# Values' and output projections of an attention and mixture-of-experts block as three half-precision products

## The chip, the cores and the metric

The kernel runs on one core of a Trainium2 chip. The metric is the device time of one execution in microseconds (us). A difference is judged against the spread of repeated runs.

## What is computed

For each of 8 sequences of 512 tokens with 256 features the reference computes attention with 32 heads of 8 features, and then a feed-forward layer with 2 shared and 16 routed experts, of which each token takes 4. A layer norm follows each of the two. Cut to what matters here:

```
q = rope(x @ Wq.T);  k = rope(x @ Wk.T);  v = x @ Wv.T
allowed = causal & (4 chunks of 32 keys, by q against the chunk's mean k)
o = softmax(where(allowed, q k' / sqrt(8), -1e30)) @ v
o = o * rsqrt(mean(o*o)) * o_norm_weight * sigmoid(x @ Wg1.T @ Wg2.T)
x = layernorm(x + o @ Wo.T)
x = layernorm(x + ffn(x))
```

q and k decide which chunks are chosen. v and Wo only scale the result.

## The kernel before

The weights stay on the chip. Eight turns follow, one for each sequence b. Turn b holds the attention of b and, woven into it, the feed-forward layer of m = b - 1. All engines run fixed programs and meet through semaphores; the order of the work is that in which each engine's program is written. A turn has these stages:

- the first products: the transpose of the normed tokens (`x1_transpose`), the transposes and chunk means of q and k, the router, and the experts' first chunks;
- the choice of chunks: DVE finds the best chunks, PE and ACT stack q and k (`stack`), and the experts' chunks 3 to 10 run beside them;
- the maxima: 40 units, in which PE makes the scores (`max_unit`) and DVE reduces them (L1346); between them the experts' chunks 11 to 21 go through PE (`up`, `down`), ACT (L834, L843), DVE (L1156) and POOL (L1045, the `low` part);
- the probabilities: 8 groups of 5 units, in which PE makes the scores again (`key_unit`, L503), ACT takes their exponentials (L986), POOL masks them (L1105) and PE multiplies by v (`outputs`, L712);
- the junction to turn b + 1, which the change touches.

In the junction PE's program is, in this order: `project_v(b + 1, 0)` (L399), `to_tokens(NG - 2)` (L722), the last group's `outputs`, `heads_out(0)` (four transposes of the gated heads, L760, into the PSUM bank `BK_AT`), `to_tokens(NG - 1)`, `project_qk` for token tiles 0 and 1 (L407), `project_v(b + 1, 1)`, `heads_out(1)` into the same bank, `project_out(0)` and `(1)` (L767), `project_qk` and `project_v` for tiles 2 and 3. In the meantime DVE normalises the last groups of heads (`two_groups`, ending in L1391), turns q and k of tiles 0 and 1 (`rope`, L1244 and L1245), adds x to the projected output (L1409), and does the layer norm (L1178 to L1188), whose result PE transposes at L512. ACT copies the transposed heads from PSUM to `aT` (`heads_copy`, L995), with the products of `turned` (L892, L893: 16 for each pair of tiles) between the copy of k = 0 and that of k = 1, and then copies v (L899).

A product of 32-bit operands stands in the trace as two MATMUL records, one of 16-bit operands as one. The experts' products already use pairs of 16-bit parts: three products (high by high, high by low, low by high) take the place of one.

At the start DVE fills a few buffers (L1132 to L1136), turns q and k of the first tiles (L1242 to L1245), and takes the low parts of the experts' weights (L1418, L1143), while PE projects sequence 0. In the last turn no next sequence is projected: PE goes from `to_tokens(NG - 1)` straight to `heads_out(1)`.

## Time and profile before

| | |
|---|---|
| median of 3 runs | 1489.6 us (1489.12 to 1492.46) |
| the profiled execution: its time, its span | 1490.47 us, 1488.7 us |
| PE busy | 1349.9 us (91%) in 11024 matmuls |
| DVE busy | 1085.1 us (73%) |
| ACT busy | 840.4 us (56%) |
| POOL busy | 533.7 us (36%) |
| mean granted TensorE clock | 0.956 |

The span is the stretch from the first to the last instruction in the trace. A busy share is a mean over stages with different limits, so what an edit is worth has to be read from the stage in which it stands. Matmuls overlap, so that PE counts as busy while it waits for little else than the end of the last one.

### The profile page before, as it was taken

How to read it: one execution, taken by the hardware profiler on the slowest of the kernel's cores; microseconds unless marked ns; L12 is line 12 of the kernel's file. 1: busy time of each engine (PE TensorE's matmuls, PEld its weight loads, DVE VectorE, ACT ScalarE, POOL GpSimd, SP SyncE). 2: the span in 40 equal slices, each digit the busy share in tenths (PEclk: the TensorE clock that was granted, in tenths of full speed). 3: DMA queues.
4: the chain of work that ended last, by engine and by line, in shares of the span. 5: the costliest groups of instructions: out<-in, count | busy, mean ns of one | idle time of the engine just before them, and what ended most of it. 6: DMA issues, size and time to landing. Idle time of an engine off the chain costs nothing.

```text
span 1488.7 us, 29120 instructions
## 1 busy us (share of the span) xinstructions
PE 1349.9 (91%) x11024; PEld 740.0 (50%) x11024; DVE 1085.1 (73%) x2746; ACT 840.4 (56%) x1266; POOL 533.7 (36%) x638
## 2 busy tenths in 40 slices
PE   5687999999998999989999999989999899999697
PEld 3322565536654465535755356543654357553364
DVE  6993679857797578966789577975789667985534
ACT  5407773396635865287733966358752776339221
POOL 3203532254223542245322553235322453225143
PEclk8657999999999999999999999999999999999799
DMA  6001031200221021210222003211112102220031
GB/s 235 15 15 16 15 91 61 51 30 23 80 70 36 25 65 57 66 31 15 87 64 51 16 23 93 64 37 30 61 56 71 31 16 72 64 52 16 16 111 60
DMA packets 52207, 77.74 MB, mean 52 GB/s; under 512 B 6322, under 2 KB 26724, under 8 KB 51812
## 3 DMA queue, kind: packets, MB, share of 16 engines
q1 hardware_dynamic: 52068, 75.89, 17.5%
q8 instruction: 87, 1.43, 0.4%
q14 instruction: 52, 0.43, 0.1%
HBM read 66.95 MB, written 8.65 MB: 51 GB/s over the span
## 4 chain that ended last, share of the span: by engine, by line
PE 54%; DVE 22%; ACT 12%; issue 4%; DVEq 3%; POOL 2%; DMA 2%; SPq 0%; POOLq 0%
PE PS L568 12%; PE PS L556 12%; DVE CM L1346 8%; ACT UQ L986 7%; PE PS L712 7%; PE PS L486 4%; DVE hr L1156 3%; PE PS L503 3%; PE PS L456 3%; ACT UK L986 2%; POOL hp L1045 2%; PE PS L767 2%; PE PS L722 2%; PE PS L407 2%; DVEq L1148 1%
## 5 line engine op out<-in xcount | busy, mean ns | idle before, releaser
L1045 POOL TENSOR_TENSOR hp<-hr,hp 128x512 f16<-128x512 f32 (+1 forms) x200 | 236.9, 1184 | 623.6 <-ACT hp L843 560.3
L1346 DVE TENSOR_REDUCE CM<-PS 128x32 f32<-128x1024 f32 x320 | 377.3, 1219 | 29.3 <-PE PS L486 25.2
L568 PE MATMUL PS<-W,hp 128*128 128x256 f16 (+1 forms) x2400 | 315.1, 274 | 16.2 <-POOL hp L1045 15.7
L556 PE MATMUL PS<-x1T,W 128*128 128x512 f16 (+1 forms) x1200 | 314.2, 389 | 0.0
L568 PEld LDWEIGHTS PS<-W,hp 128*128 128x128 f16 (+1 forms) x2400 | 214.2, 98 | 104.0 <-POOL hp L1045 38.2
L843 ACT ACTIVATE hp<-hr 128x512 f16<-128x512 f32 (+1 forms) x178 | 112.7, 633 | 247.2 <-DVE hr L1156 229.7
L834 ACT ACTIVATE hr<-PS,CF 128x512 f32<-128x512 f32 (+1 forms) x200 | 137.0, 685 | 198.3 <-PE PS L556 193.0
L1156 DVE TENSOR_TENSOR hr<-hr,gB 128x512 f32<-128x512 f32 x176 | 126.1, 717 | 103.0 <-ACT hr L834 99.7
L556 PEld LDWEIGHTS PS<-x1T,W 128*128 128x128 f16 (+1 forms) x1200 | 108.7, 100 | 115.0 <-issue 38.7
L986 ACT ACTIVATE UK<-PS 128x1024 f32<-128x1024 f32 x160 | 153.4, 1041 | 10.8 <-PE PS L503 10.5
L986 ACT ACTIVATE UQ<-PS 128x1024 f32<-128x1024 f32 x160 | 150.4, 1042 | 1.6
L503 PE MATMUL PS<-qET,kz 64*128 64x512 f16 (+3 forms) x1024 | 111.5, 304 | 27.5 <-ACT UK L986 12.0
L486 PE MATMUL PS<-kz,qET 64*128 64x512 f16 (+3 forms) x1024 | 132.5, 318 | 0.0
L1105 POOL TENSOR_SCALAR_AFFINE_SELECT UK<-UK 128x512 f32<-128x512 f32 x128 | 78.6, 639 | 148.3 <-ACT UK L986 148.3
L503 PEld LDWEIGHTS PS<-qET,kz 64*128 64x128 f16 x1024 | 32.1, 94 | 165.8 <-ACT UQ L986 70.3
L1364 DVE COPY ropeb<-PS 128x512 f32<-128x512 f32 x64 | 44.3, 692 | 93.8 <-PE PS L712 93.6
L1105 POOL TENSOR_SCALAR_AFFINE_SELECT UQ<-UQ 128x512 f32<-128x512 f32 x128 | 78.8, 640 | 65.9 <-ACT UQ L986 65.9
L712 PE MATMUL PS<-UK,vst 128*9 128x512 f32 (+3 forms) x1024 | 87.6, 437 | 0.0
L712 PE MATMUL PS<-UQ,vst 128*9 128x512 f32 (+3 forms) x1024 | 83.9, 434 | 0.0
L930 ACT ACTIVATE kz<-PS 128x1024 f16<-128x1024 f16 x64 | 65.2, 1018 | 6.8 <-PE PS L456 6.8
L477 PE MATMUL PS<-CG 128*128 128x256 bf16 x256 | 52.2, 288 | 17.1 <-DVE CM L1346 16.9
L933 ACT ACTIVATE qET<-PS 128x1024 f16<-128x1024 f16 x64 | 65.7, 1027 | 0.0
(149 smaller groups left out, 1803.4 us busy)
## 6 DMA issues: line engine op xcount, KB each, us to landing
gB<-gates SPq DMA_DIRECT2D x64, 256.0 KB, 3.2
gB<-gates SPq DMA_DIRECT2D x32, 224.0 KB, 2.9
gB<-gates SPq DMA_DIRECT2D x32, 192.0 KB, 2.9
gB<-gates SPq DMA_DIRECT2D x32, 160.0 KB, 2.5
xT<-in_xT SPq DMA_DIRECT2D x8, 512.0 KB, 5.5
qET<-rows SPq DMA_DIRECT2D x16, 256.0 KB, 5.4
v<-in_x SPq DMA_DIRECT2D x8, 512.0 KB, 4.1
gB<-gates SPq DMA_DIRECT2D x32, 128.0 KB, 2.9
```

The lines of the kernel that those rows point to most:

```text
L486: mm = pe.matmul(PS[:, r + half, o:o + w], qET[rows, a, t * P:(t + 1) * P], kz[rows, a, 0:w], start=False, stop=True, skip_group_check=Tru ...
L503: mm = pe.matmul(PS[:, r + half, o:o + w], kz[rows, a, t * P:(t + 1) * P], qET[rows, a, t * P:S], start=True, stop=True, tile_position=(64 ...
L556: mm = pe.matmul(PS[0:w, BK_H[c % 2], :], W1[:, a, k, bass.ds(f0, w)], x1T[:, e, k, :], start=(n == 0), stop=(n == 5))
L568: mm = pe.matmul(PS[:, BK_Y + j // 2, (j % 2) * D:(j % 2 + 1) * D], hp[0:w, slot, a, j * P:(j + 1) * P], W2[0:w, e, bass.ds(c, 1), :].rear ...
L712: mm = pe.matmul(PS[32 * hh:32 * hh + HD + 1, BK_PV, t * P:S], vst[:, gs % 2, t, hh, :], PT[gs % 2][:, hh, o:o + w], start=(n == 0), stop= ...
L834: nc.scalar.activation(hr[0:w, slot, :], PS[0:w, BK_H[c % 2], :], ACT.Relu, bias=bias).then_inc(act_h, 1)
L843: nc.scalar.activation(hp[0:w, slot, 0, :], hr[0:w, slot, :], ACT.Copy).then_inc(s_high, 1)
L986: nc.scalar.activation(dst, src, ACT.Exp, scale=SCALE).then_inc(act_p, 1)
L1045: nc.gpsimd.tensor_tensor(hp[0:w, slot, 1, :], hr[0:w, slot, :], hp[0:w, slot, 0, :], ALU.subtract).then_inc(pool_hp, 1)
L1105: nc.gpsimd.affine_select(block, block, [[0, HG], [1, P]], ALU.is_ge, zero, base=0, channel_multiplier=-1).then_inc(pool_p, 1)
L1156: nc.vector.tensor_tensor(hr[:, slot, :], hr[:, slot, :], gB[:, r, :], ALU.mult).then_inc(dve_h, 1)
L1346: nc.vector.tensor_reduce(dst, src, AX.X, ALU.max).then_inc(dve_cm, 1)
```

## The change

The projection of v and the output projection, so far one product of 32-bit operands for each token tile and half of the contraction, become three products of 16-bit parts. The weights are multiplied by 64 before they are split, and the results divided by 64 as they leave PSUM (in ACT's copy of v and in DVE's addition of x). The parts of the weights are made once, at the start, by DVE and ACT, in the place of the 32-bit weights, with 64 times the weights held for a time in the unused end of `kz`. The input is split for each sequence: `high_x` on ACT and `low_x` on POOL, behind chunks 5 and 6 of the maxima of the turn before, and at the start for sequence 0. The transposed heads are split by `heads_copy` on ACT (high) and a new `heads_low` on DVE (low), which reads the PSUM bank as well. The projections of q and k stay as they are. At the start they now stand ahead of those of v.

```diff
@@ -49,6 +49,8 @@
+WIDE = 64.0
@@ -131,6 +133,7 @@
+        xTp = sb("xTp", [P, 2, KT, S], F16)
@@ -156,9 +159,12 @@
-        aT = qf[:, 0:1024].rearrange("p (k s) -> p k s", k=KT)
+        aTp = qf[:, 0:1024].bitcast(F16).rearrange("p (e k s) -> p e k s", e=2, k=KT)
         ropew = qf[:, 1024:3072].rearrange("p (t c) -> p t c", t=NT)
         kz = sb("kz", [P, H // 2, S], F16)
+        wide_w = kz[:, :, :].rearrange("p a s -> p (a s)").bitcast(F32)[:, 12 * D:16 * D].rearrange("p (n k d) -> p n k d", n=2, k=KT)
+        WVp = WA[:, :, 2 * D:3 * D].bitcast(F16).rearrange("p k (e d) -> p e k d", e=2)
+        WOp = WO[:, :, :].bitcast(F16).rearrange("p k (e d) -> p e k d", e=2)
@@ -394,15 +405,17 @@
                 if j == 0:
-                    pe.wait_ge(s_xT, 16 * b + 16)
-                for k in range(KT):
-                    mm = pe.matmul(PS[:, BK_Y + j // 2, (j % 2) * D:(j % 2 + 1) * D], xT[:, k, j * P:(j + 1) * P],
-                                   WA[:, k, 2 * D:3 * D], start=(k == 0), stop=(k == KT - 1))
+                    pe.wait_ge(act_xh, b * KT + KT)
+                    pe.wait_ge(pool_xl, b * KT + KT)
+                for n, (k, a, e) in enumerate((k, a, e) for k in range(KT) for a, e in ((0, 0), (0, 1), (1, 0))):
+                    mm = pe.matmul(PS[:, BK_Y + j // 2, (j % 2) * D:(j % 2 + 1) * D], xTp[:, a, k, j * P:(j + 1) * P],
+                                   WVp[:, e, k, :], start=(n == 0), stop=(n == 3 * KT - 1))
...
+                pe.wait_ge(s_xT, 16 * b + 16)
@@ -410,8 +423,10 @@
                 for j in range(first, last):
+                    project_qk(b, j)
+                pe.wait_ge(dve_wide, 2)
+                for j in range(first, last):
                     project_v(b, j)
-                    project_qk(b, j)
@@ -755,7 +770,7 @@
                     if k:
-                        pe.wait_ge(act_aT, b * KT + k)
+                        pe.wait_ge(dve_aT, b * KT + k)
@@ -763,11 +778,16 @@
-                    for j in range(NT):
-                        mm = pe.matmul(PS[:, 4 + j // 2, (j % 2) * D:(j % 2 + 1) * D], aT[:, k, j * P:(j + 1) * P],
-                                       WO[:, k, :], start=(k == 0 and j % 2 == 0), stop=(k == KT - 1), skip_group_check=True)
-                        if j % 2 and k == KT - 1:
-                            mm.then_inc(pe_att, 1)
+                    for a, parts in ((0, (0, 1)), (1, (0,))):
+                        if a:
+                            pe.wait_ge(dve_aT, b * KT + k + 1)
+                        for j in range(NT):
+                            for e in parts:
+                                mm = pe.matmul(PS[:, 4 + j // 2, (j % 2) * D:(j % 2 + 1) * D], aTp[:, a, k, j * P:(j + 1) * P],
+                                               WOp[:, e, k, :], start=(k == 0 and a == 0 and j % 2 == 0 and e == 0),
+                                               stop=(k == KT - 1 and a == 1), skip_group_check=True)
+                            if j % 2 and k == KT - 1 and a == 1:
+                                mm.then_inc(pe_att, 1)
@@ -814,6 +834,15 @@
+            def high_x(b, k):
+                act.wait_ge(s_xT, 16 * b + 16)
+                nc.scalar.activation(xTp[:, 0, k, :], xT[:, k, :], ACT.Copy).then_inc(act_xh, 1)
+            for k in range(KT):
+                high_x(0, k)
+            act.wait_ge(dve_wide, 1)
+            nc.scalar.activation(WVp[:, 0], wide_w[:, 0], ACT.Copy).then_inc(act_wide, 1)
@@ -897,7 +926,7 @@
-                                     ACT.Copy).then_inc(act_v, 1)
+                                     ACT.Copy, scale=1.0 / WIDE).then_inc(act_v, 1)
@@ -945,6 +974,8 @@
+                        if more and u in (5, 6):
+                            high_x(b + 1, u - 5)
@@ -992,7 +1023,7 @@
-                    nc.scalar.activation(aT[:, k, :], PS[:, BK_AT, :], ACT.Copy).then_inc(act_aT, 1)
+                    nc.scalar.activation(aTp[:, 0, k, :], PS[:, BK_AT, :], ACT.Copy).then_inc(act_aT, 1)
@@ -1014,6 +1045,8 @@
+            act.wait_ge(dve_wide, 3)
+            nc.scalar.activation(WOp[:, 0], wide_w[:, 1], ACT.Copy).then_inc(act_wide, 1)
@@ -1034,6 +1067,13 @@
+            def low_x(b, k):
+                pool.wait_ge(act_xh, b * KT + k + 1)
+                nc.gpsimd.tensor_tensor(xTp[:, 1, k, :], xT[:, k, :], xTp[:, 0, k, :], ALU.subtract).then_inc(pool_xl, 1)
+            for k in range(KT):
+                low_x(0, k)
@@ -1082,12 +1122,16 @@
-                    for (first, last), steps in ((C_TOPK, NG // 2), (C_MAX, MAX_STEPS)):
-                        n = (last - first) // steps
-                        pool.drain()
-                        for i in range(0, steps):
-                            for u in range(n):
-                                low(m, i * n + first + u, (first + u) % 2)
+                    pool.drain()
+                    for c in range(*C_TOPK):
+                        low(m, c, c % 2)
+                    pool.drain()
+                for u, c in enumerate(range(*C_MAX)):
+                    if m is not None:
+                        low(m, c, c % 2)
+                    if more and u in (5, 6):
+                        low_x(b + 1, u - 5)
+                if m is not None:
@@ -1129,6 +1173,9 @@
+            nc.vector.tensor_scalar(wide_w[:, 0], WA[:, :, 2 * D:3 * D], WIDE, None, ALU.mult).then_inc(dve_wide, 1)
+            dve.wait_ge(act_wide, 1)
+            nc.vector.tensor_tensor(WVp[:, 1], wide_w[:, 0], WVp[:, 0], ALU.subtract).then_inc(dve_wide, 1)
@@ -1307,7 +1354,8 @@
-                    nc.vector.tensor_scalar(WO[:, :, :], WO[:, :, :], onw, None, ALU.mult).then_inc(dve_w, 1)
+                    dve.wait_ge(act_wide, 2)
+                    nc.vector.tensor_tensor(WOp[:, 1], wide_w[:, 1], WOp[:, 0], ALU.subtract).then_inc(dve_w, 1)
@@ -1399,15 +1447,22 @@
+                def heads_low(k):
+                    dve.wait_ge(act_aT, b * KT + k + 1)
+                    nc.vector.tensor_tensor(aTp[:, 1, k, :], PS[:, BK_AT, :], aTp[:, 0, k, :], ALU.subtract).then_inc(dve_aT, 1)
+                heads_low(0)
                 if more:
                     rope(b + 1, 0, 2)
+                heads_low(1)
...
-                    nc.vector.tensor_tensor(x1n[:, 2 * i:2 * i + 2, :].rearrange("p t d -> p (t d)"), PS[:, 4 + i, :],
-                                            x[:, 2 * i:2 * i + 2, :].rearrange("p t d -> p (t d)"), ALU.add).then_inc(dve_x1, 1)
+                    nc.vector.scalar_tensor_tensor(out=x1n[:, 2 * i:2 * i + 2, :].rearrange("p t d -> p (t d)"), in0=PS[:, 4 + i, :],
+                                                   scalar=1.0 / WIDE, in1=x[:, 2 * i:2 * i + 2, :].rearrange("p t d -> p (t d)"),
+                                                   op0=ALU.mult, op1=ALU.add).then_inc(dve_x1, 1)
@@ -1416,6 +1471,8 @@
+            dve.wait_ge(s_small, 16 * N_SMALL)
+            nc.vector.tensor_scalar(wide_w[:, 1], WO[:, :, :], onw, WIDE, ALU.mult, ALU.mult).then_inc(dve_wide, 1)
...

```

PE's program in the junction, from `project_v(b + 1, 0)` on, with the products of v (L399) and of the output (L767); before:

```order
L399 MATMUL PS<-WA,xT 128x256 x2
L760 MATMUL PS<-CF,qT 128x128 [waits act_aT,dve_on,act_p]
L760 MATMUL PS<-CF,qT 128x128 x3
L767 MATMUL PS<-WO,qET 128x256 [waits dve_otok,act_aT]
L767 MATMUL PS<-WO,qET 128x256 x3
L767 MATMUL PS<-WO,qET 128x256 [waits dve_otok,act_aT]
L767 MATMUL PS<-WO,qET 128x256 x3
```

and in the changed kernel, where these lines are L411, L775 and L786:

```order
L411 MATMUL PS<-WA,xTp 128x256 x6
L775 MATMUL PS<-CF,qT 128x128 [waits dve_aT,dve_on,act_p]
L775 MATMUL PS<-CF,qT 128x128 x3
L786 MATMUL PS<-WO,qET 128x256 [waits dve_otok,act_aT]
L786 MATMUL PS<-WO,qET 128x256 x7
L786 MATMUL PS<-WO,qET 128x256 [waits dve_aT]
L786 MATMUL PS<-WO,qET 128x256 x3
L786 MATMUL PS<-WO,qET 128x256 [waits dve_otok,act_aT]
L786 MATMUL PS<-WO,qET 128x256 x7
L786 MATMUL PS<-WO,qET 128x256 [waits dve_aT]
L786 MATMUL PS<-WO,qET 128x256 x3
```

Every row of order counts instructions of the program, of which a 32-bit product is one. Eight output products have become 24, and PE now waits for DVE (`dve_aT`) at three places: ahead of the second set of transposes, and ahead of the low products of each k.

DVE's program in the same place, from the last instruction of the gated heads (the first row) to the addition of x (the last two); before:

```order
L1391 SCALAR_TENSOR_TENSOR qT<-qT,CM 128x4x64
L1244 TENSOR_TENSOR UK<-UK,qET 128x64x4 [waits act_rope]
L1245 TENSOR_TENSOR UK<-UK,qET 128x64x4
L1244 TENSOR_TENSOR UK<-UK,qET 128x64x4 [waits act_rope]
L1245 TENSOR_TENSOR UK<-UK,qET 128x64x4
L1409 TENSOR_TENSOR x1n<-PS,v 128x512 [waits pe_att,s_x]
L1409 TENSOR_TENSOR x1n<-PS,v 128x512 [waits pe_att]
```

and in the changed kernel:

```order
L1439 SCALAR_TENSOR_TENSOR qT<-qT,CM 128x4x64
L1452 TENSOR_TENSOR qET<-PS,qET 128x512 [waits act_aT]
L1291 TENSOR_TENSOR UK<-UK,qET 128x64x4 [waits act_rope]
L1292 TENSOR_TENSOR UK<-UK,qET 128x64x4
L1291 TENSOR_TENSOR UK<-UK,qET 128x64x4 [waits act_rope]
L1292 TENSOR_TENSOR UK<-UK,qET 128x64x4
L1452 TENSOR_TENSOR qET<-PS,qET 128x512 [waits act_aT]
L1463 SCALAR_TENSOR_TENSOR x1n<-PS,v 128x512 [waits pe_att,s_x]
L1463 SCALAR_TENSOR_TENSOR x1n<-PS,v 128x512 [waits pe_att]
```

The two new instructions (L1452) stand in the row between the gated heads and the addition: one ahead of the turning of q and k, one behind it.

## Rows read from the trace of the kernel before

**Rows 1.** Windows: stretch, length, busy us (instructions) of PE, PEld, DVE, ACT, POOL, clock, DMA

```profile
403.00:458.00 55.00, 51.81 (x403) 27.19 (x404) 51.20 (x51) 15.54 (x23) 11.55 (x10) 1.00 0.18 59
475.00:508.00 33.00, 31.27 (x356) 9.96 (x358) 19.04 (x59) 32.79 (x36) 19.18 (x36) 1.00 0.08 27
```

**Rows 2.** Timeline, junction of turn 2: start, length, engine, line, operation, count [idle before]

```profile
508.32 1.13 PE L399 MATMUL PS<-WA,xT 128*128 128x256 f32 x4
508.45 0.69 DVE L1364 COPY ropeb<-PS 128x512 f32<-128x512 f32 x1 [0.64 <-PE PS L712]
...
516.90 1.03 PE L399 MATMUL PS<-WA,xT 128*128 128x256 f32 x4
517.32 0.42 DVE L1391 SCALAR_TENSOR_TENSOR qT<-qT,CM 128x256 f32<-128x256 f32 x1
517.85 0.63 PE L760 MATMUL PS<-CF,qT 128*128 128x128 f32 x4
519.42 0.76 ACT L995 ACTIVATE qET<-PS 128x512 f32<-128x512 f32 x1
520.12 0.42 DVE L1245 TENSOR_TENSOR UK<-UK,qET 128x256 f32<-128x256 f32 x1
520.23 1.59 PEld L767 LDWEIGHTS PS<-WO,qET 128*128 128x128 f32 x8 [0.43 <-ACT qET L995]
521.50 1.46 DVE L1409 TENSOR_TENSOR x1n<-PS,v 128x512 f32<-128x512 f32 x2 [0.95 <-PE PS L767]
...
528.51 1.10 PE L512 MATMUL PS<-CF,x1n 128*128 128x128 f32 x8 [1.13 <-DVE x1n L1188]
```

**Rows 3.** The chain that ended last, merged: start, length, what

```profile
344.66 3.47 PE PS L767 x16
...
368.90 2.73 PE PS L568 x24
```

**Rows 4.** Groups by line and shape: busy us, mean ns | idle before

```profile
L1194 DVE TENSOR_TENSOR x1T<-PS,x1T 128x512 f16<-128x512 f32 x16 | 10.4, 686 | 2.6 <-ACT x1T L855 2.0
L1223 DVE SCALAR_TENSOR_TENSOR x1n<-x1n,PS 128x512 f32<-128x512 f32 x16 | 10.3, 684 | 34.5 <-PE PS L568 34.5
```

**Rows 5.** Timeline, the addition of x in the junction of turn 1

```profile
347.39 1.46 DVE L1409 TENSOR_TENSOR x1n<-PS,v 128x512 f32<-128x512 f32 x2 [1.01 <-PE PS L767]
```

**Rows 6.** Timeline, the last turn's output projection

```profile
1389.51 5.29 PE L767 MATMUL PS<-WO,qET 128*128 128x256 f32 x16
```

**Rows 7.** Timeline, the start

```profile
8.39 0.48 DVE L1132 MEMSET PS<- 128x512 f32 x1 [8.39 <-DMA CG<-in_cg]
9.59 0.20 ACT L815 ACTIVATE hr<-CF 128x1 f32<-128x1 f32 x1
10.48 0.40 DVE L1136 TENSOR_SCALAR cbias<-CF 128x512 f16<-128x512 f32 x1
16.50 0.69 DVE L1242 TENSOR_TENSOR ropeb<-PS,CF 128x512 f32<-128x512 f32 x1 [0.59 <-PE PS L407]
18.72 3.46 DVE L1418 TENSOR_TENSOR W<-UK,W 128x3168 f16<-128x3168 f32 x1
```

**Rows 8.** Timeline, the maxima of turn 2

```profile
423.83 4.61 DVE L1346 TENSOR_REDUCE CM<-PS 128x32 f32<-128x1024 f32 x4
423.94 0.63 ACT L843 ACTIVATE hp<-hr 128x512 f16<-128x512 f32 x1 [2.79 <-DVE hr L1156]
424.65 1.16 POOL L1045 TENSOR_TENSOR hp<-hr,hp 128x512 f16<-128x512 f32 x1 [3.71 <-ACT hp L843]
```

**Rows 9.** Windows just behind a junction, columns as in rows 1

```profile
531.00:536.00 5.00, 5.00 (x47) 3.53 (x46) 3.42 (x19) 2.41 (x6) 2.49 (x3) 0.67 0.00 0
1054.00:1058.00 4.00, 4.00 (x49) 3.38 (x49) 2.45 (x11) 2.65 (x6) 2.27 (x2) 1.00 0.00 0
```

**Rows 10.** Timeline, the addition of x in two other junctions

```profile
871.22 1.46 DVE L1409 TENSOR_TENSOR x1n<-PS,v 128x512 f32<-128x512 f32 x2 [0.95 <-PE PS L767]
1044.48 1.46 DVE L1409 TENSOR_TENSOR x1n<-PS,v 128x512 f32<-128x512 f32 x2 [0.95 <-PE PS L767]
```

More of the change, by code:

```diff
@@ L267, in build @@
         act_aT = sem("act_aT")
+        dve_aT = sem("dve_aT")
+        dve_wide = sem("dve_wide")
+        act_wide = sem("act_wide")
+        act_xh = sem("act_xh")
+        pool_xl = sem("pool_xl")
         pe_att = sem("pe_att")
@@ L1046, in low, with turn @@
                                         ALU.subtract).then_inc(pool_hp, 1)
-            def turn(b, m):
+            def turn(b, m, more):
                 def stack_low(j, n):
@@ L1116, in turn @@
                 causal(NG - 1, 1)
-            turn(0, None)
+            turn(0, None, True)
             for b in range(1, B - 1):
-                turn(b, b - 1)
-            turn(B - 1, B - 2)
+                turn(b, b - 1, True)
+            turn(B - 1, B - 2, False)
             for c in range(NC):
```

## The prediction

> **What bounds the kernel now.** I read the profile from the whole to the place of the change. The table of busy times makes PE look like the limit (91%), and the change takes work from PE, so I first asked in which stage PE's time counts. The windows by stage answer that. In the maxima DVE is busy 51.2 of 55 us, and in the probabilities ACT 32.79 of 33 us [rows 1]; PE's high share there is a matmul counted as busy while it waits its turn. Only between a junction and the maxima is PE itself the limit, and the change touches no product there. What it makes faster stands in the junction, so I read the timeline of one junction instruction by instruction, asking of each product which wait ends last in front of it and behind it.
>
> **What is saved on PE.** A 32-bit output product of 256 columns is two records, and 16 records took 3.47 us: 0.434 us for a product. 24 products of 16-bit parts with 256 columns took 2.73 us: 0.114 us each, 0.341 us for three [rows 3]. So a product that becomes three saves 0.093 us. With 8 of v and 8 of the output for each sequence that is 16 x 0.093 = 1.5 us a turn, 12 us in all, if all of it lay on the path. It does not:
>
> - v, tile 0: its two products start at 508.32 and take 0.87 us, to 509.19. Behind them `to_tokens` needs DVE's copy, which ends at 508.45 + 0.69 = 509.14 [rows 2]. Only 0.05 us comes free.
> - v, tile 1: it starts at 516.90 and would end 0.19 us earlier than 517.77. The transposes of `heads_out(1)` behind it wait for DVE's L1391, which ends at 517.74, and start at 517.85 [rows 2]. Nothing comes free but 0.03 us.
> - v, tiles 2 and 3: PE idles 1.13 us behind them, until DVE's layer norm is there at 528.51 [rows 2]. The 0.37 us saved becomes more idle time.
>
> I take 0.07 us a junction for all of it, seven junctions: -0.5 us. The lower bound, every saving on v real, is 8 x 0.093 x 7 = -5.2 us.
>
> **What the output projection becomes.** Before, the addition of x starts when four records of the second half (k = 1) are through; the second half waits for ACT's copy, which ends at 519.42 + 0.76 = 520.18, and the addition starts at 521.50, 1.32 us later [rows 2]. In the changed kernel the low products of k = 1 stand last, and wait for `heads_low(1)` on DVE. For that instruction I take the nearest row, L1194: the same shapes, PSUM and a 16-bit tile in, 16 bit out, 0.69 us [rows 4]. Step by step:
>
> 1. `heads_low(0)` stands behind L1391 on DVE, from 517.84 to 518.53, though its input was there long before. The second transposes now wait for it, since they overwrite its bank: they start at 518.6 in place of 517.85, take 0.63 us [rows 2], and ACT can have them at about 519.3. ACT is busy with `turned` until 519.42 [rows 2], so this 0.7 us is hidden, by 0.1 us.
> 2. DVE finishes the turning of q and k at 520.12 + 0.42 = 520.54 [rows 2]; ACT's copy for k = 1 is there at 520.18. `heads_low(1)` runs from 520.6 to 521.3.
> 3. PE has begun the output products at about 519.1 (0.5 us behind the transposes, an estimate from their 0.63 with the drain off), and has done the first 20 of 24 by 519.1 + 20 x 0.114 = 521.4. The low products of k = 1 start then; two are needed for the first half of the addition. The second starts at 521.5, takes some 0.27 us like other 16-bit products of this size (an estimate from the spacing, 0.114 us, and the drain that the last of such a row shows) and 0.15 us to reach DVE: the addition starts at 521.95 in place of 521.50.
>
> That is +0.45 us. The addition itself costs nothing more: L1223, the same kind of instruction as the new one, takes 0.684 us for the same shape, and L1409's two take 1.46 [rows 4, 2]. Behind the addition stands the layer norm, and behind it PE, idle; so the 0.45 us is passed on whole. Bounds: 0 if PE gets its release sooner than I think, and 0.9 us if `heads_low` is slowed to the 0.76 us of ACT's copy beside it and the hidden 0.7 us shows in part.
>
> Six junctions have this form. In that of turn 1 ACT was free earlier and PE set the pace: 16 records without a pause from 344.66 on, addition at 347.39 [rows 3, 5], 2.73 us later. There the start moves by the 0.75 us that `heads_low(0)` costs, and to the release it is 21 x 0.114 + 0.42 = 2.8 us, nothing less than before, because all low products stand at the end: +0.6 to 0.8, I take +0.6. In the last turn PE has no other work and runs at the 1.2 GHz level for part of it: the 16 records take 5.29 us, drain and all [rows 6], where 3.47 went by above. The 0.75 us comes in front, and of 24 products against 16 records of about equal length at that level little is won: +0.4, between 0 and 1.2. Junctions together: 6 x 0.45 + 0.6 + 0.4 = +3.7 us.
>
> **The start.** DVE's four fills run from 8.39 to 10.88, and it then waits for PE [rows 7]. Now it first scales the weights, waits for ACT and takes the low part. ACT is free at 9.79 [rows 7] and has three copies of 128x512 ahead, two of x and one of the weights, at 0.63 each (L843's price) [rows 8]: 11.7. DVE's subtraction, 0.69 [rows 4], ends at 12.4, the fills 2.49 later, at 14.9. From the second turning (16.50) to the next instruction (18.72) it is 2.22 us [rows 7]; two of them from 14.9 end at 19.3 in place of 18.72: +0.6. Behind it come the scaling of Wo, at most 0.69 us, and a subtraction in the place of a multiplication, some 0.2 us more. DVE has hardly a pause until the first maxima, so I count +1.2 us, between 0.4 and 2.2.
>
> **In the maxima** ACT gets two copies (0.63 us) and POOL two subtractions (1.16 us) for each sequence. ACT idles 2.79 us before L843, POOL 3.71 us before L1045 in each round of one chunk [rows 8]; they fit. DVE, which is the limit here, does four reductions in 4.61 us while POOL's instruction runs beside them [rows 8], 1.15 us each: it isn't held up. Were that cover gone, it would cost 2 x 1.16 us in 7 turns, 16 us. The Trainium skill ("SBUF — State Buffer", SBUF: two separate sides) says of the port pair that DVE and GpSimd share that it is an exclusive lock, and that the loser waits for the whole instruction; it limits this to DVE operations in certain modes or with two SBUF inputs. By the lock in full the sum would be those 16 us more; by the row it is nothing, and the row decides, as the reductions read PSUM.
>
> **Sum:** -0.5 + 3.7 + 1.2 = +4.4 us.
>
> **The clock.** PE runs behind a junction at either of two levels. Just behind that of turn 2 the mean granted clock is 0.67, so part of the stretch stood at 1.2 GHz; behind that of turn 5 it is 1.00 [rows 9]. The drop follows the idle time before the transposes and a run of small products. Its price from two periods between additions of x: 521.50 - 347.39 = 174.11 us, and in the turn without a drop 1044.48 - 871.22 = 173.26 [rows 2, 5, 10]: 0.85 us. The trace has it behind four of the seven junctions. PE's idle time there, 1.13 us, grows by 0.45 + 0.37 to about 2 us, so I expect at least one more: +0.9. The Trainium skill ("TensorE: Matmul & The Clock Gate", Why this matters for your kernels) warns of idle gaps longer than this one would be; by that rule a gap of 2 us costs nothing and the sum stays 4.4. The trace is against reading it so narrowly, since the clock fell behind a gap of 1.13 us.
>
> The forecast is 4.4 + 0.9 = +5.3 us. The profiled execution took 1490.47 us for a span of 1488.7, 0.9 us above the median of 1489.6. On its own time the sum gives 1495.8; on the median, 1494.9. I give the latter.
>
> **Rivals.**
> - *PE's savings count after all* (faster): in the junction PE would have to be the limit from the second transposes on. If DVE reached `heads_low` without delaying PE, both the output's 8 x 0.093 and v's would come through, 1.5 us a turn, and even with the start's 1.2 it would be about 1479. For it: PE has hardly a gap in the timeline there. Against it: each of the four places above has a wait for DVE or ACT ending within 0.1 us of PE's own end, and the low products stand last. It decides where `heads_low(1)` ends before 520.5 and L1391 before 517. Chance 0.07.
> - *No change*: the waits of `heads_low` are hidden more than I find (0 to 0.1 a junction), the start costs 0.5, and the clock drops as often as before, or in fewer places: between 1487 and 1492.5. Chance 0.18.
> - *The clock falls behind all seven junctions*, and the first turn and the last one, both partly at 1.2 GHz, lose a stretch more: 4.4 + 3 x 0.85 + 2 = +9, about 1498.5. For it: more idle time in every junction. Against it: the drop also hangs on something that the rows don't show, since equal junctions differ. Chance 0.2.
> - *The forecast*, 1492.6 to 1497: chance 0.5.
> - *More than that*, with `heads_low` waiting behind ACT and rope at the upper bounds (0.9 a junction), 1500 and over: 0.05.
>
> **Chances and range.** A measurement of this kernel tells 0.2% (3 us) from no change. Faster by over that: 0.08; within it, 0.19; slower, 0.73. The range leaves the savings case and the last one outside: 1490 to 1499.5. The forecast's own is 1492.6 to 1497.
>
> **What the changed profile would show.** The group of the v products: 24 for each sequence, mean near 0.27 us. In the junction the second transposes released by DVE, 0.7 us later after L1391 than now; the low products of k = 1 released by DVE; the addition of x some 0.45 us later after ACT's copy than 1.32 us. PE idle before the transposes of the normed tokens 2 us in place of 1.13. The first large subtraction of DVE at about 19.3. The forecast would be wrong if DVE's `heads_low` took much less than 0.69 us or found its input late, if the maxima grew from 55 us, or if the granted clock in the windows behind the junctions changed level in more or fewer than five places.

## The result, and the profile after

The changed kernel took 1500.94 us (median of 4 runs, 1497.46 to 1502.84), the kernel before on the same chip 1490.65 us (4 runs). The ratio is 1.0061, 95% interval [1.0043, 1.0078]: slower by about 9 us. The profiled execution of the changed kernel took 1497.46 us for a span of 1495.5 us, 6.8 us more than the span before; it is the fastest of the four, so the profile shows less of the loss than the median. Of all executions of the kernels below one, of the changed kernel with 7 fillers, stands apart at 4340 us, and its ratio leaves it out.

The page's busy times of the changed kernel, and its row of TensorE's granted clock:

```profile
PE 1338.9 (90%) x11152; PEld 730.0 (49%) x11152; DVE 1094.5 (73%) x2765; ACT 849.8 (57%) x1284; POOL 551.4 (37%) x654
PEclk8757999999999999999999999999999999999798
```

PE did 128 matmuls more and was busy 11.0 us less, as the price of a product in parts says, and the kernel is slower. The timeline of the junction of turn 2 answers to [rows 2]:

```profile
519.71 0.82 PE L411 MATMUL PS<-WA,xTp 128*128 128x256 f16 x6
520.13 0.43 DVE L1439 SCALAR_TENSOR_TENSOR qT<-qT,CM 128x256 f32<-128x256 f32 x1
520.65 0.69 DVE L1452 TENSOR_TENSOR qET<-PS,qET 128x512 f16<-128x512 f32 x1
521.49 0.63 PE L775 MATMUL PS<-CF,qT 128*128 128x128 f32 x4 [0.96 <-DVE qET L1452]
521.95 2.86 PE L786 MATMUL PS<-WO,qET 128*128 128x256 f16 x24
522.23 0.76 ACT L1026 ACTIVATE qET<-PS 128x512 f16<-128x512 f32 x1
523.45 0.69 DVE L1452 TENSOR_TENSOR qET<-PS,qET 128x512 f16<-128x512 f32 x1
524.19 0.33 PEld L786 LDWEIGHTS PS<-WO,qET 128*128 128x128 f16 x4 [0.18 <-DVE qET L1452]
524.73 1.29 DVE L1463 SCALAR_TENSOR_TENSOR x1n<-PS,v 128x512 f32<-128x512 f32 x2 [0.59 <-PE PS L786]
528.08 1.47 PE L411 MATMUL PS<-WA,xTp 128*128 128x256 f16 x12
531.49 1.54 PE L527 MATMUL PS<-CF,x1n 128*128 128x128 f32 x8 [1.94 <-DVE x1n L1235]
```

ACT's copy of k = 1 ends at 522.99 and the addition starts at 524.73, 1.74 us later, where it was 1.32: +0.42. PE now waits 0.96 us for `heads_low(0)`, and 1.94 us ahead of the transposes of the normed tokens instead of 1.13. In the other six junctions this wait was 0.78 or 0.79 us and is now 1.65 to 1.69, behind turn 6 2.02. Two windows of the maxima and the probabilities of turn 2 answer to [rows 1] (columns as there):

```profile
405.84:460.84 55.00, 51.82 (x404) 27.18 (x405) 51.20 (x51) 16.59 (x25) 13.77 (x12) 1.00 0.19 58
477.84:510.84 33.00, 31.27 (x357) 9.96 (x358) 19.02 (x59) 32.79 (x36) 19.12 (x36) 1.00 0.08 26
```

DVE is busy for 51.20 us as before, beside two ACT copies and two POOL subtractions more. The start and the last turn, in the timeline (they answer to [rows 7] and [rows 6]):

```profile
19.12 3.46 DVE L1473 TENSOR_TENSOR W<-UK,W 128x3168 f16<-128x3168 f32 x1
1396.33 1.08 PE L775 MATMUL PS<-CF,qT 128*128 128x128 f32 x4 [5.04 <-DVE qET L1452]
1397.20 5.32 PE L786 MATMUL PS<-WO,qET 128*128 128x256 f16 x24
```

The other difference is in the clock. Windows of 10.2 us from the start of the transposes (L527) on, behind four of the seven junctions of the changed kernel:

```profile
182.10:192.30 10.20, 9.32 (x83) 7.29 (x84) 7.57 (x33) 6.17 (x12) 3.79 (x4) 1.00 0.01 2
531.50:541.70 10.20, 10.20 (x80) 8.68 (x80) 6.62 (x30) 6.27 (x12) 3.43 (x3) 0.83 0.01 2
882.20:892.40 10.20, 10.20 (x79) 8.13 (x80) 7.66 (x33) 6.16 (x12) 4.05 (x4) 0.83 0.01 2
1231.40:1241.60 10.20, 10.20 (x80) 8.69 (x80) 6.67 (x29) 6.27 (x12) 3.42 (x3) 0.83 0.00 0
```

A mean of 0.83 is a stretch at 1.2 GHz in a window that is at 2.4 GHz otherwise. In this execution five of the seven junctions have it, in that of before four; the third window here, behind turn 4, was at 1.00 before. The first row below lies in the stretch behind turn 2. The other two are stretches at the beginning of the exponentials of turns 1 and 4, which had none before:

```profile
532.80:535.60 2.80, 2.80 (x17) 2.80 (x15) 1.49 (x3) 2.54 (x7) 2.01 (x2) 0.54 0.02 6
304.00:307.00 3.00, 3.00 (x20) 0.26 (x12) 1.45 (x7) 2.68 (x4) 1.13 (x3) 0.55 0.00 0
829.50:832.00 2.50, 2.50 (x16) 0.29 (x18) 1.50 (x7) 2.20 (x4) 1.19 (x3) 0.50 0.00 0
```

One more difference of the clock stands in the probabilities of turn 0. The first turn runs at 1.2 GHz for a long time in every kernel, and in the changed one this lasts some 3 us longer. The same window of the kernel before and of the changed one, in this order:

```profile
128.00:134.00 6.00, 5.97 (x60) 1.66 (x60) 0.69 (x1) 5.87 (x7) 3.76 (x8) 0.84 0.01 3
```
```profile
128.00:134.00 6.00, 5.69 (x48) 1.06 (x46) 0.05 (x1) 5.01 (x6) 3.48 (x7) 0.61 0.01 3
```

### The profile page after: what moved, and what is told of

It reads as the page before. It is cut to its first block, busy times and chain, and to the rows that moved or that the text cites. A ratio compares the mean times of both kernels' runs of the same rounds, so it can differ in the third digit from the quotient of the medians.

```text
span 1495.5 us, 29430 instructions
## 1 busy us (share of the span) xinstructions
PE 1338.9 (90%) x11152; PEld 730.0 (49%) x11152; DVE 1094.5 (73%) x2765; ACT 849.8 (57%) x1284; POOL 551.4 (37%) x654
## 4 chain that ended last, share of the span: by engine, by line
PE 51%; DVE 25%; ACT 11%; issue 5%; DVEq 4%; POOL 2%; DMA 2%; SPq 0%; POOLq 0%; ACTq 0%
PE PS L583 12%; PE PS L571 11%; DVE CM L1394 8%; PE PS L727 7%; ACT UQ L1017 7%; PE PS L501 4%; PE PS L518 3%; DVE hr L1203 3%; PE PS L471 3%; ACT UK L1017 2%; POOL hp L1085 2%; PE PS L737 2%; DVEq L1195 2%; PE PS L786 1%; ACT hp L872 1%
## 5 line engine op out<-in xcount | busy, mean ns | idle before, releaser
L571 PE MATMUL PS<-x1T,W 128*128 128x512 f16 (+1 forms) x1200 | 310.5, 385 | 0.0
L492 PE MATMUL PS<-CG 128*128 128x256 bf16 x256 | 52.1, 288 | 17.2 <-DVE CM L1394 17.0
L420 PE MATMUL PS<-WA,xT 128*128 128x512 f32 x128 | 59.9, 613 | 8.4 <-DMA CG<-in_cg 8.4
```

The costliest lines, as they stand in the source:

```text
L571: mm = pe.matmul(PS[0:w, BK_H[c % 2], :], W1[:, a, k, bass.ds(f0, w)], x1T[:, e, k, :], start=(n == 0), stop=(n == 5))
```

## The experiments

Four questions, in this order: which part costs; is it work on the path or the clock; is it the place of PE's idle time or its amount; does idle time alone do it. A filler is a product whose result nobody uses. At the end of the section a table sets the runs beside PE's idle time. Every ratio is to the kernel before.

**1. Each part alone.** One kernel keeps v in parts and has the output projection in 32 bits as before; the other the reverse.

```diff
 # v only: output projection as before
-                    for a, parts in ((0, (0, 1)), (1, (0,))):
...
+                    for j in range(NT):
+                        mm = pe.matmul(PS[:, 4 + j // 2, (j % 2) * D:(j % 2 + 1) * D], aT[:, k, j * P:(j + 1) * P],
+                                       WO[:, k, :], start=(k == 0 and j % 2 == 0), stop=(k == KT - 1), skip_group_check=True)
...
-                heads_low(0)
-                heads_low(1)
 # output only: v as before
-                for n, (k, a, e) in enumerate((k, a, e) for k in range(KT) for a, e in ((0, 0), (0, 1), (1, 0))):
+                for k in range(KT):
```

> Only the projection of v is split; the output projection is the 32-bit one of before, without heads_low. Theory A (the loss is the wait for heads_low on DVE, 0.4 us a junction, plus the later start): the additions of x come at the same distance behind the copy of the heads as before (1.3 us), and what is left is the start, so 0.5 to 1.5 us over before. Theory B (the loss is above all in stretches at 1.2 GHz, brought on by more idle time of PE): v's three products still leave PE idle longer ahead of the transposes of the normed tokens (1.5 in place of 1.1 us), so this kernel loses 2 to 4 us.

> Only the output projection is split; v stays 32-bit, so nothing is split in the maxima and nothing waits at the start but for Wo. Theory A: 0.4 x 7 + 1 in the last turn = +3.8 us, and almost nothing at the start. Theory B: PE's idle time ahead of the transposes grows by the 0.4 us of the wait alone, and the loss is 5 us or more. Theory C (the splitting of x in the maxima and at the start costs more than I counted): this kernel is within 4 us of before, and the kernel with v alone has the rest of the 10 us.

v alone: 1.0000 [0.9991, 1.0008]. The output alone: 1.0003 [0.9993, 1.0014]. Neither part costs anything that can be told, and both together cost 0.6%. By the upper ends of the two intervals the parts come to 1.2 + 2.1 = 3.3 us at most, and the change costs 6.4 at least. So the parts don't add up, and something which depends on both is at work. The output alone came out below what theories A and B expected, and theory C failed too, as v alone doesn't have the rest.

**2. The low products of k = 1.** The changed kernel, with only k = 0 of the output projection in parts and no `heads_low(1)`:

```diff
-                    for a, parts in ((0, (0, 1)), (1, (0,))):
+                    for a, parts in ((0, (0, 1)), (1, (0,))) if k == 0 else ():
...
+                    for j in range(NT) if k else ():
+                        mm = pe.matmul(PS[:, 4 + j // 2, (j % 2) * D:(j % 2 + 1) * D], aT1[:, j * P:(j + 1) * P],
+                                       WO[:, k, :], start=False, stop=True, skip_group_check=True)
...
-                heads_low(1)
```

> The changed kernel, but in the output projection only the first half of the contraction (k = 0) is split; k = 1 is a 32-bit product again, so heads_low(1) is gone and nothing behind ACT's copy waits for DVE. Theory A: the addition of x comes 1.3 us behind the end of ACT's copy again, 0.4 us a junction sooner than in the changed kernel, 3 us in all. Theory B: PE has less idle time too, fewer drops, and 4 to 7 us come back.

1.0013 [1.0004, 1.0022]. From the first exponential of turn 2 (472.91) to the addition (523.46) it took 50.55 us, in the changed kernel 50.85 (473.88 to 524.73), before 50.46 (471.04 to 521.50). So `heads_low(0)` costs 0.1 us in this stretch, and three quarters of the 0.4 us hang on the last four products and `heads_low(1)`. On the path that is 0.3 x 7 = 2.1 us, but the whole kernel is 6 us faster than the changed one, as theory B said. PE's idle time ahead of the transposes is down to 1.20 to 1.54 us as well, and no junction has a stretch at 1.2 GHz longer than those above.

**3. The start.** DVE does its four fills ahead of the low part of v's weights, not behind it:

```diff
-            dve.wait_ge(act_wide, 1)
-            nc.vector.tensor_tensor(WVp[:, 1], wide_w[:, 0], WVp[:, 0], ALU.subtract).then_inc(dve_wide, 1)
 # the same two lines, behind the four fills
+            dve.wait_ge(act_wide, 1)
+            nc.vector.tensor_tensor(WVp[:, 1], wide_w[:, 0], WVp[:, 0], ALU.subtract).then_inc(dve_wide, 1)
```

> The changed kernel, but at the start DVE does its four fills while ACT makes the high parts, and takes the low part of v's weights behind them. Theory A: the first turning of q and k is no longer later than its product (14.7 becomes about 13.0), so 0.4 us of the start's 0.8 come back, in the time too if nothing else moves. Theory B: the same 0.4 us, hidden by differences of 1 to 3 us between executions.

1.0051 [1.0035, 1.0066], not told apart from the changed kernel. The first large subtraction started at 17.97, earlier than in either kernel, and the first exponential at 123.65, as in the changed one (123.70; before 123.11). The order on DVE at the start doesn't set the time of the first exponential.

**4. The changed kernel once more**, to see whether the profile of the first run had shown all.

> The changed kernel once more, unaltered, beside the same before as the three below. After the first four kernels (v alone 1.0000 of before, output alone 1.0003, both with fillers 1.0023), theory A (a sum of the two parts) gives at most 1.001; theory B (both parts bring on stretches at 1.2 GHz that neither brings on alone) gives 1.004 to 1.007, with a trace that has other drops than the first one's, since nothing in the kernel fixes where they fall.

1.0055 [1.0040, 1.0070]. The profiled execution had a span of 1500.9 us, and windows around the junction of turn 2 show what the first profile lacks:

```profile
532.80:542.20 9.40, 9.40 (x62) 7.93 (x61) 5.02 (x24) 4.39 (x10) 3.42 (x3) 0.50 0.01 2
543.00:548.00 5.00, 5.00 (x32) 2.50 (x30) 4.68 (x41) 2.72 (x7) 3.38 (x3) 1.00 0.03 7
```

PE stands at 1.2 GHz for all of 9.4 us, not for some 3. I call these stretches short and long from here on. That turn took 177.34 us from addition to addition, against 174.9. The profiled executions of steps 3, 5 (the last turn alone) and 6, which leave this idle time as it is or 0.1 us longer, have one long stretch each, too; that of step 3 behind turn 2, that of step 5 behind turn 6:

```profile
532.80:542.20 9.40, 9.40 (x61) 7.93 (x60) 5.04 (x24) 4.47 (x10) 3.42 (x3) 0.50 0.01 2
```
```profile
1231.90:1241.30 9.40, 9.40 (x60) 7.93 (x59) 5.14 (x26) 4.60 (x11) 3.24 (x3) 0.50 0.00 0
```

The long stretch isn't what makes this execution 5.4 us longer than the first, though. The spans by stage, each added up over the turns:

| stage, us | before | changed | changed again |
|---|---|---|---|
| start, to the first reduction | 65.9 | 66.4 | 66.5 |
| first reduction to first exponential | 533.8 | 533.4 | 533.4 |
| first exponential to addition of x | 405.9 | 412.7 | 411.9 |
| addition to transposes | 47.1 | 46.1 | 46.2 |
| transposes to first reduction | 341.4 | 343.7 | 344.9 |
| behind the last addition | 94.6 | 93.3 | 98.2 |

At the last addition the two are 0.5 us apart (1402.24 and 1402.78). The other 4.9 us lie behind it, where the second execution stands at 1.2 GHz once more (a window of each, the first execution first):

```profile
1416.00:1426.00 10.00, 7.35 (x50) 4.32 (x48) 2.40 (x7) 4.78 (x9) 3.07 (x3) 1.00 0.27 80
```
```profile
1419.80:1429.80 10.00, 8.72 (x35) 4.88 (x36) 0.46 (x1) 1.81 (x3) 0.37 (x1) 0.50 0.40 108
```

So one execution says little about the place of some 5 us, and the experiments go by medians.

**5. Filling the idle time.** Ahead of `x1_transpose` in the order of PE's program go n small 16-bit products into a PSUM bank that nobody reads at that time (the work isn't used):

```diff
+                pe.wait_ge(dve_x1, 2 * b + 3)
+                for _ in range(7 if more else 12):
+                    pe.matmul(PS[:, 4, :], W1[:, 0, 0, 0:P], W1[:, 0, 0, 0:S], start=True, stop=True)
```

On the changed kernel with 7 in each of seven junctions and 12 in the last turn (as shown), with 2 and none, 9 and 20, and none and 12; on the kernel before with 4 and 12; on v alone with 6 and 12:

> The changed kernel, with 7 products of 512 columns (16-bit, 0.22 us each, results thrown away) that fill PE's idle time ahead of the transposes of the normed tokens, 12 in the last turn. Theory B: fewer stretches at 1.2 GHz behind the junctions, and 3 to 6 us faster than the changed kernel (1500.9), the last turn's transposes at 2.4 GHz among it. Theory A: the clock has no part in it, the fillers are hidden in a wait for DVE, and the time is that of the changed kernel within 1 us.

> The changed kernel with 2 filler products of 256... columns' 16-bit kind (0.43 us together) into a bank that nobody reads, on PE ahead of the transposes of the normed tokens in seven junctions, none in the last turn; idle time there from 1.94 to about 1.5 us. Theory A: as the changed kernel (1.0055 of before, within 0.1%). Theory B: part of what 7 fillers gave back, 1 to 3 us less than the changed kernel, ratio 1.0035 to 1.005.

> The changed kernel with 9 such fillers in each of seven junctions (about 1.9 us, all of the gap) and 20 in the last turn. Theory A: nothing is given back, or up to 1.4 us more is lost where fillers run past the layer norm's end. Theory B: at least as fast as with 7 and 12 (ratio 1.0023), 1.001 to 1.0025, unless they run past the end by 0.2 us a junction (1.4 us, then 1.003).

> The changed kernel with 12 fillers in the last turn alone and none in the seven junctions. It splits what 7 and 12 fillers gave back (4.5 us). Theory B, by the junctions: the last turn's part is 1.5 us at most, ratio 1.0045 to 1.0055, and the granted clock still falls behind the junctions as in the changed kernel. Rival: the whole comes from the last turn, ratio 1.0023 to 1.003.

> The kernel before, with 4 such fillers (0.9 us) ahead of the transposes of the normed tokens, 12 in the last turn. Theory B: the drops behind the junctions (0.85 us each, four in the execution profiled) become fewer, 2 to 5 us faster than before. Theory A: no change, within 1 us.

> v alone split, with 6 fillers of 512 columns (1.3 us) in the 1.5 us that PE idles ahead of the transposes of the normed tokens, 12 in the last turn. Theory B: fewer drops than the five of v alone, 0.85 us for each: 0.997 to 0.999 of before, the first version that beats both. Theory A: 1.000.

Changed kernel: 7 and 12 give 1.0023 [1.0014, 1.0032], 2 and none 1.0033 [1.0020, 1.0045], 9 and 20 1.0031 [1.0021, 1.0042], the last turn alone 1.0076 [1.0064, 1.0089]. So more work on PE gives back 3 to 6 us, in the seven junctions; two products do nearly what seven or nine do, a little more than expected; nine and 20 came out as was expected if they run past the layer norm's end; and fillers in the last turn alone give nothing back (their ratio is above both expectations). On the kernel before 0.9987 [0.9975, 0.9999], the only version whose interval lies below 1, by 2 us; on v alone 0.9998 [0.9987, 1.0010], no gain.

On these last two the expectation of fewer stretches failed. PE idles 0.26 us at most ahead of the transposes, and the profiled executions have short stretches behind four and five of the seven junctions, as many as without fillers (the kernel before with fillers, then v alone with fillers, behind turn 2):

```profile
528.10:538.30 10.20, 10.17 (x79) 7.80 (x80) 7.84 (x36) 6.16 (x12) 4.04 (x4) 0.83 0.01 2
```
```profile
532.10:542.30 10.20, 10.20 (x79) 8.25 (x80) 7.85 (x37) 6.16 (x12) 4.10 (x4) 0.83 0.01 2
```

Of the 3.1 us that the profiled execution of the kernel before gains by its fillers, 0.6 are there at the last addition (1393.45 against 1394.07); the rest lies behind it. So the short stretches of these two kernels don't hang on this idle time.

**6. The same two products in another place**, ahead of `heads_out(1)`, where PE waits for `heads_low(0)`:

```diff
+                if more:
+                    pe.wait_ge(dve_otok, (b + 1) * NG + 1)
+                    for _ in range(2):
+                        pe.matmul(PS[:, 4, :], W1[:, 0, 0, 0:P], W1[:, 0, 0, 0:S], start=True, stop=True)
                 heads_out(1)
```

> The changed kernel with 2 fillers (0.43 us together) in seven junctions, not in the idle time ahead of the transposes of the normed tokens but ahead of the second transposes of the heads, where PE waits 0.96 us for DVE; the idle time ahead of the later transposes stays at 1.94 us. Theory C (the gap ahead of the transposes): nothing is given back, 1.0055 to 1.0065. Theory D (the amount of PE's work in the junction): as 2 fillers in the other place, 1.0033.

1.0046 [1.0029, 1.0064]: between the two expectations, and its interval holds both. The profiled execution has a long stretch behind turn 2. Inconclusive.

**7. Less work.** If the idle time is the cause, taking products away must cost time. v's second half of the contraction is left out for some token tiles, in four kernels:

```diff
 # kernel before: v in 32 bits, tiles 2 and 3
+                ks = (0,) if j >= 2 else range(KT)
+                for k in ks:
...
 # output in parts, v in 32 bits, tile 3;   v in parts alone, tile 3:   j == 3
 # changed kernel: v in parts, tiles 2 and 3
+                ks = (0,) if j >= 2 else range(KT)
+                for n, (k, a, e) in enumerate((k, a, e) for k in ks for a, e in ((0, 0), (0, 1), (1, 0))):
...
```

> The kernel before, in which the projection of v for token tiles 2 and 3 of every sequence takes only the first half of the contraction (k = 0); the second half is left out, so v isn't v there. That takes two 32-bit products (2 x 0.43 us) from PE ahead of the transposes of the normed tokens, nothing else moves, and PE's idle time there should be 1.13 + 0.87 = 2.0 us, about that of the changed kernel. Theory A (the time of the change is only the work that DVE and PE got on the path): the same time as before, within 1 us, since only idle time grows. Theory B (the idle time ahead of the transposes lets the granted clock fall behind it more often, or for longer): 2 to 5 us slower than before, with more or longer stretches at 1.2 GHz behind the junctions, though there is less work.

> Only v split, the output projection in 32 bits as before, and of v for token tile 3 the second half of the contraction left out (so v isn't v there): PE's idle time ahead of the transposes goes from 1.5 to about 1.85 us. Theory C: no cost, as v alone, 0.999 to 1.001. If idle time of this length costs behind any junction but that of the kernel before: 1.002 to 1.005.

> Only the output projection split, v in 32 bits as before, and of v for token tile 3 the second half of the contraction left out (so v isn't v there). It has the changed kernel's junction (the low parts of the heads, their waits) and, with 0.43 us taken from PE behind it, PE's idle time ahead of the transposes of the normed tokens goes from about 1.6 to 2.0 us, the changed kernel's. Theory C (that idle time costs clock only behind the split output projection): as the changed kernel, 1.004 to 1.0065. Theory D (it takes both parts of the change, since the amount of work on PE in the whole junction counts): near the split output alone (1.0003), 1.000 to 1.002.

> The changed kernel in which v for token tiles 2 and 3 takes only the first half of the contraction (the other half is left out, so v isn't v there): six 16-bit products less on PE ahead of the idle time, which grows from 1.94 to about 2.6 us. If the cost grows with the idle time: slower than the changed kernel though it does less, 1.007 to 1.009. If it is a threshold that the changed kernel has passed: the same, 1.0055 to 1.0065.

In the kernel before: 1.0007 [0.9999, 1.0016], though PE idled 1.99 us ahead of the transposes of turn 2 and 1.65 ahead of the others, as in the changed kernel. Idle time of this length alone doesn't cost what the changed kernel loses, and the expectation from the clock failed here. v alone: 1.0007 [0.9999, 1.0016]. Output alone: 1.0026 [1.0015, 1.0038], between the two expectations, where it cost nothing without the cut. The changed kernel: 1.0130 [1.0114, 1.0145], 19 us slower than before, and 10 to 11 slower than with the six products a junction; that is more than either expectation. In the timeline PE's work in the junction, and the first reduction of the maxima:

```profile
533.32 0.82 PE L412 MATMUL PS<-WA,xTp 128*128 128x256 f16 x6
536.74 1.09 PE L528 MATMUL PS<-CF,x1n 128*128 128x128 f32 x8 [2.60 <-DVE x1n L1236]
...
588.76 4.62 DVE L1395 TENSOR_REDUCE CM<-PS 128x32 f32<-128x1024 f32 x4 [0.16 <-issue]
```

and windows around that junction, and of 10.2 us behind two others:

```profile
533.00:538.00 5.00, 2.40 (x20) 1.75 (x17) 4.16 (x20) 3.77 (x15) 0.00 (x0) 1.00 0.01 2
538.60:548.30 9.70, 9.70 (x60) 8.14 (x59) 5.60 (x28) 5.00 (x10) 3.29 (x4) 0.50 0.01 2
549.00:554.00 5.00, 5.00 (x35) 2.45 (x33) 4.62 (x35) 2.93 (x6) 2.69 (x4) 1.00 0.03 8
181.70:191.90 10.20, 10.16 (x68) 8.46 (x69) 6.21 (x27) 4.83 (x10) 3.42 (x3) 0.57 0.01 2
713.90:724.10 10.20, 10.16 (x79) 8.27 (x80) 7.59 (x32) 6.16 (x12) 3.67 (x4) 0.83 0.01 2
```

Behind six of the seven junctions the mean of the 10.2 us is 0.56 or 0.57, behind turn 3 it is 0.83. From the transposes to the first reduction it takes 52.02 us (588.76 - 536.74). Over all kernels this part of a turn takes 48.2 to 48.9 us where the window stands at 1.00, 49.0 to 49.5 at 0.83, and 51.9 to 52.1 with a long stretch. That prices a short stretch at some 0.9 us and a long one at 3 to 3.8.

**8. The same, filled.** The last kernel with 9 fillers in each of seven junctions, and 12 in the last turn:

> The changed kernel without the second half of the contraction of v for token tiles 2 and 3 (left out, so v isn't v there), as in the run that came out at 1.0130, and now with 9 fillers (1.9 us) in each of seven junctions in the idle time of 2.6 us, 12 in the last turn. If the idle time ahead of the transposes is the cause: 1.002 to 1.0035, as the changed kernel with fillers, and no stretch of 10.2 us at 1.2 GHz behind a junction. If leaving the products out is the cause in another way: 1.010 to 1.013.

1.0015 [1.0006, 1.0024]. The 1.3% is down to 0.15%, a little below the expectation, and what came back is 17 us, for 63 products in the junctions that nobody uses (the 12 in the last turn gave nothing back in step 5). Two windows behind junctions, as above:

```profile
181.40:191.60 10.20, 10.20 (x79) 7.97 (x80) 7.57 (x33) 6.16 (x12) 3.80 (x4) 0.83 0.01 2
356.00:366.20 10.20, 9.57 (x85) 7.33 (x85) 7.85 (x36) 6.16 (x12) 4.03 (x4) 1.00 0.01 2
```

None of the seven has a long stretch; three stand at 1.00. PE's idle time ahead of the transposes, added up over the kernel by the view of their line for PE alone, for the kernels before, changed, cut and filled in this order (each line from its own kernel's view: us, waits):

```profile
  DVE x1n L1188: 11.8, 8
```
```profile
  DVE x1n L1235: 18.5, 8
```
```profile
  DVE x1n L1236: 23.4, 8
```
```profile
  DVE x1n L1239: 5.7, 8
```

One of the eight waits is that of the last turn, 5.9 to 6.5 us, or less with fillers there (2.4 with 12). The table leaves it out. Its last column counts the stretches at 1.2 GHz behind the seven junctions, short and long, in the profiled execution.

| kernel | idle, us, seven junctions | ratio | short, long |
|---|---|---|---|
| before | 5.9 | 1 | 4, 0 |
| before with fillers | 0.3 | 0.9987 | 4, 0 |
| before with the cut | 11.9 | 1.0007 | 4, 0 |
| v alone; with fillers | 8.8; 0.3 | 1.0000; 0.9998 | 5, 0; 5, 0 |
| v alone with the cut | 11.1 | 1.0007 | 6, 0 |
| output alone; with the cut | 9.5; 12.6 | 1.0003; 1.0026 | 4, 0; 4, 0 |
| k = 0 of the output, and v | 9.1 | 1.0013 | 5, 0 |
| changed (two runs) | 12.3; 12.3 | 1.0061; 1.0055 | 5, 0; 3, 1 |
| changed, fills first | 12.3 | 1.0051 | 4, 1 |
| changed, fillers in the last turn alone | 12.9 | 1.0076 | 3, 1 |
| changed, fillers ahead of `heads_out(1)` | 12.3 | 1.0046 | 2, 1 |
| changed with 2, 7, 9 fillers | 9.3; 1.8; 0.1 | 1.0033; 1.0023; 1.0031 | 3, 0; 2, 0; 2, 0 |
| changed with the cut | 17.0 | 1.0130 | 1, 6 |
| changed with the cut and 9 fillers | 3.4 | 1.0015 | 4, 0 |

Short stretches come with every idle time, the filled one too. Long ones don't: all ten stand behind idle times of 1.92 us or more. In the five executions of the changed kernel and its variants with 12.3 or 12.9 us, four of the ten junctions with 1.92 to 2.12 us have one, and none of the 25 with 1.65 to 1.77; with the cut it is six of seven, at 2.31 to 2.69. In the other forms of the junction only three idle times are that long (1.99 in the kernel before with the cut, 2.04 and 2.05 in the output alone with the cut), and none has a long stretch behind it. That is too few to say that they couldn't.

In the changed form a longer idle time costs more from 9.3 us on, and below that the time doesn't follow it. Between forms it doesn't order the kernels: at 11.9 us the old junction costs 1 us, at 12.3 us the new one costs 8 to 9, of which 3 to 5 stay when the gap is filled.

## Why the prediction failed, step by step

- **PE's savings lie in front of waits:** right. v alone gives 1.0000, and PE's 11.0 us less of busy time bought nothing.
- **The junction, +0.45:** right, and it measured +0.42. The second transposes started 0.93 us behind the end of DVE's gated heads (521.49 against 520.13 + 0.43), before 0.11, as `heads_low(0)` stands between; that was hidden, as predicted. The new instruction took 0.69 us, as its nearest row [rows 4]. The addition lasts 1.29 us, not 1.46 [rows 2]: its two halves follow each other closer, 0.17 us back in each junction that I had not counted.
- **Turn 0,** counted among the six junctions of this form: first exponential to addition took 51.90 us (123.70 to 175.60) against 50.81 before (123.11 to 173.92), +1.09. The longer first stretch at 1.2 GHz lies there. In the execution with 7 fillers, in which it is as short as before, it took 50.69. The kernel before with the cut has the longer one too (51.80), so it isn't shown that the change brings it.
- **Turn 1, +0.6:** there the profile shows the new stretch at 1.2 GHz as well. In the execution of the changed kernel with the cut, which has none there, first exponential to addition took 51.16 us (301.62 to 352.78) against 50.51 before (296.88 to 347.39): +0.65.
- **The last turn, +0.4 (0 to 1.2):** above its bound in both executions of the changed kernel: first exponential to addition 53.57 us (1348.67 to 1402.24), before 52.21 (1341.86 to 1394.07), so +1.36. Kernels with the same last turn took 52.3 to 54.0, so this part moves with the execution. The part behind the last addition, for which the prediction has no term, was 1.3 us shorter in the first execution and 3.6 longer in the second.
- **The start, +1.2 (0.4 to 2.2):** at the low bound. The large subtraction starts 0.40 later, the first exponential 0.59.
- **The maxima, 0:** right: 51.20 us of DVE as before, and from the first reduction to the first exponential of turn 2 67.83 us in both kernels.
- **The clock:** the step that failed is "PE's idle time there, 1.13 us, grows by 0.45 + 0.37 to about 2 us, so I expect at least one more: +0.9." The idle time came out as said (1.94), though 1.13 was that of turn 2 alone, and that of the others was 0.79. In the first profiled execution one more junction fell, as said, but that was luck: in the kernel before and in v alone a filled gap left as many short stretches (in the changed kernel two or three), so their number doesn't follow from the idle time. The premise "The drop follows the idle time before the transposes" fails for the short stretches, and the term was sized by them, as the trace of before had no others behind a junction. What the longer idle time brings is the long stretch, at 3 to 3.8 us instead of 0.9. Fillers that change only PE's idle time gave back 3 to 6 us, and left 1.0023 to 1.0033, 3.4 to 4.9 us, which is about the sum of 4.4 for all but the clock. That this sum fits is in part luck too, as 0.17 us a junction less and more in turn 0 and the last turn stand against each other. The clock's term is thus some 3 to 6 us, not 0.9.
- **The rival of seven junctions** had +9 in all, near the measured loss, by a count that didn't occur: five junctions, then four. The other half of it, that the first turn and the last one lose a stretch more, is in the profiles, the first turn's in both executions, the last one's in the second.

The rule of the Trainium skill that I weighed ("TensorE: Matmul & The Clock Gate", Why this matters for your kernels) warns of longer idle gaps than these, so that by it they would cost nothing. The runs are against that: gaps of 1.92 to 2.69 us came with long stretches at 1.2 GHz, and filling them took these away.

**Shown:** in the new junction the idle time ahead of the transposes is a cause, since taking products away cost 10 us and brought six long stretches, and filling the gap gave back 3 to 6 us and 17, with no long stretch left in the four executions profiled. **Open:** whether the old junction would have long stretches too if more of its idle times were 2 us, or what in the new one takes part. The new one has a second wait on PE (0.96 us ahead of `heads_out(1)`) and 16-bit products for 32-bit ones, but the run that filled the second wait was inconclusive, and what distinguishes the two was not isolated. Open is also what the short stretches follow.

## What to carry to other kernels

Work taken from an engine that then only waits longer was not free on PE here: look at the granted clock behind each gap, and price the gap that you are about to widen by a run with more and with less in it, not by the stretches that the kernel already has. Two parts of a change that cost nothing alone can cost together, so a term that depends on a level must not be added up from its parts. A few unused products in the gap are a cheap test of what of a loss hangs on the gap; what lies elsewhere, as the short stretches here, they leave. And compare medians: two executions of the same kernel differed by 5 us, most of it far from the change.

## What the runs showed that I had not expected

- Leaving out six small products in each of seven junctions made the kernel 10 to 11 us slower (1.0061 to 1.0130), and 63 unused ones made that kernel 17 us faster (1.0015).
- Stretches at 1.2 GHz came in two lengths behind the same junction, in executions of the same kernel: some 3 us in one and over 9.4 us in another, at some 0.9 and 3.8 us of time.
- Two products (0.43 us) gave back nearly as much as seven: 1.0033 and 1.0023.
- With the gap filled, the short stretches behind the junctions of the kernel before and of v alone were as many as without.
